# Graph attention with residual and layer norm on one core: the first adjacency columns are loaded ahead of x's last chunk, the row constant is made before the first scores, and masks are made later in periods 0 to 4

## What is computed

```python
q = x @ Wq.T + bq
k = x @ Wk.T + bk
v = x @ Wv.T + bv
scores = q @ k.T / sqrt(128)
scores = where(adj > 0, scores, -9e15)      # adj is 4096 x 4096 int32
att = softmax(scores, axis=-1) @ v
out = layernorm(x + elu(att))
```

## Time and profile before

| | |
|---|---|
| time, median of 3 runs | 429.18 us (428.96 to 430.1) |
| the profiled execution's own time | 429.98 us |
| its span | 428.2 us |
| busy: PE, PEld (weight loads) | 415.1 us (97%), 310.7 us |
| busy: DVE, ACT, POOL | 361.7 us (84%), 353.8 us (83%), 353.5 us (83%) |
| HBM read, written | 69.47 MB, 2.10 MB |

### The profile page before, as it was taken

The page is one execution under the profiler, slowest core; times in us unless marked ns, Lnnn a source line. Parts: engine busy times, 40 slices in busy tenths (PEclk is TensorE's granted clock), DMA queues, the critical chain, the costliest instruction groups (busy, mean ns, idle before and its releaser), DMA issues.

```text
span 428.2 us, 11461 instructions
## 1 busy us (share of the span) xinstructions
PE 415.1 (97%) x3470; PEld 310.7 (73%) x3470; DVE 361.7 (84%) x677; ACT 353.8 (83%) x742; POOL 353.5 (83%) x644
## 2 busy tenths in 40 slices
PE   7897999999999999999999999999999999999994
PEld 6663777777777777777777777777777777777784
DVE  3698999888888898888888988888889888888784
ACT  5887778988888889888888898888888988888892
POOL 0588469888898898888988988889888988898875
PEclk9999999999999999999999999999999999999998
DMA  8953999999999999999999999999999999999551
GB/s 229 383 199 63 266 251 282 268 260 273 281 250 265 277 262 257 251 283 261 251 257 283 263 256 252 277 263 261 251 280 261 261 246 281 263 258 233 104 97 27
DMA packets 149649, 104.77 MB, mean 245 GB/s; under 512 B 132738, under 2 KB 141444, under 8 KB 141444
## 3 DMA queue, kind: packets, MB, share of 16 engines
q1 hardware_dynamic: 149200, 104.41, 91.6%
q10 hardware_dynamic: 436, 0.20, 0.2%
HBM read 69.47 MB, written 2.10 MB: 167 GB/s over the span
## 4 chain that ended last, share of the span: by engine, by line
POOL 58%; issue 18%; PE 11%; ACT 3%; DVE 3%; POOLq 2%; DMA 2%; SPq 2%; ACTq 0%; DVEq 0%
POOL p_rows L403 26%; POOL res L417 6%; POOL var_eps L439 4%; POOL rstd L441 4%; POOL y L422 3%; POOL att_sum L410 3%; POOL neg_mean L428 3%; PE ps_out L960 3%; POOL att L412 3%; POOL expm L419 2%; POOL centred L430 2%; DMA adj<-in_adj_dram 2%; POOL y_out L445 2%; PE ps_out L962 1%; PE ps_t L937 1%
## 5 line engine op out<-in xcount | busy, mean ns | idle before, releaser
L403 POOL TENSOR_TENSOR p_rows<-scores,p_rows 128x256 f16<-128x256 f32 x252 | 177.1, 733 | 7.4 <-ACT p_rows L560 7.0
L687 DVE CUSTOM_DVE_ANT_0 scores<-ps_scores,adj 128x1024 f32<-128x1024 f32 x128 | 155.7, 1216 | 11.6 <-issue 8.6
L543 ACT ACTIVATE scores<-scores,neg_max 128x1024 f32<-128x1024 f32 x128 | 145.9, 1140 | 4.0 <-DVE neg_max L697 4.0
L673 DVE TENSOR_SCALAR adj<-adj 128x1024 f32<-128x1024 int32 x128 | 104.3, 816 | 2.5 <-DMA adj<-in_adj_dram 2.5
L703 DVE TENSOR_TENSOR p_lo<-ps_t,p_hi 128x512 f16<-128x512 f32 x124 | 82.4, 684 | 28.4 <-ACT p_hi L552 28.3
L921 PE MATMUL ps_scores<-k_hi,q_hi 128*128 128x512 f16 x256 | 97.1, 379 | 1.1 <-DVE max_parts L687 0.7
L922 PE MATMUL ps_scores<-k_lo,q_hi 128*128 128x512 f16 x256 | 97.0, 379 | 0.0
L923 PE MATMUL ps_scores<-k_hi,q_lo 128*128 128x512 f16 x256 | 97.0, 379 | 0.0
L960 PE MATMUL ps_out<-v_parts,p_hi 128*128 128x256 f16 x496 | 95.1, 273 | 0.0
L960 PE MATMUL ps_out<-v_parts,p_turned 128*128 128x256 f16 x496 | 95.0, 273 | 0.0
L962 PE MATMUL ps_out<-v_parts,p_lo 128*128 128x128 f16 x496 | 88.5, 219 | 0.0
(11 more groups left out here) (121 smaller groups left out, 477.0 us busy)
## 6 DMA issues: line engine op xcount, KB each, us to landing
adj<-in_adj_dram SPq DMA_DIRECT2D x64, 1024.0 KB, 5.3
out_dram<-y_out SPq DMA_DIRECT2D x32, 64.0 KB, 4.8
x_rows<-in_x_dram SPq DMA_DIRECT2D x4, 256.0 KB, 4.6
x_rows<-in_x_dram SPq DMA_DIRECT2D x2, 512.0 KB, 7.1
p_turned<-p_rows SPq DMA_TRANSPOSE x63, 4.5
w_rows<-in_L_gnn_Wq_dram ACTq DMA_DIRECT2D x1, 64.0 KB, 2.8
w_rows<-in_L_gnn_Wk_dram ACTq DMA_DIRECT2D x1, 64.0 KB, 3.4
w_rows<-in_L_gnn_Wv_dram ACTq DMA_DIRECT2D x1, 64.0 KB, 4.6
```

The lines of the kernel that those rows point to most:

```text
L403: last = nc.gpsimd.tensor_tensor(p_rows[c][:, w:][:, cols], s_sb[s][:, c * PIECE:c * PIECE + w][:, cols], p_rows[c][:, 0:w][:, cols], ALU. ...
L543: nc.scalar.activation(s_sb[s][:, cols], s_sb[s][:, cols], ACT.Exp, bias=neg_max[:, s:s + 1], accum_out=p_sums[:, s, c:c + 1]).then_inc(ex ...
L673: nc.vector.tensor_scalar(mask_sb[s][:, cols], adj_sb[s][:, cols], 0.0, MASKED / SCALE, ALU.is_le, ALU.mult).then_inc(mask_ready, 1)
L687: nc.vector.tensor_tensor_reduce(out=s_sb[s][:, cols], in0=ps_scores[c % 2][:, :], in1=mask_sb[s][:, cols], scale=SCALE, scalar=-3.0e38, o ...
```

## The change

On SP, the first five x chunks are issued, then columns 0 to 1023 and 1024 to 2047 of tile 0 as two loads of 512 KB, then x's last chunk, then the other three adjacency halves of tiles 0 and 1, and bv last. On DVE and PE, the constant of the rows (`bk_wide`, the product, `row_b`) comes before PE's `transpose_x(4)`. On DVE, the mask and the masking of piece 0 of tile 0 come before `low_of_k(4)`. From period 0 to period 4 a table says which mask pieces follow each masked piece; period 4 and 5 are written out, and the loop begins at period 6.

```diff
+X_EARLY = 5
...
-            for n, (begin, end) in enumerate(X_CHUNKS):
+            def load_x(n):
+                begin, end = X_CHUNKS[n]
                 tiles = slice(begin * BLOCKS, end * BLOCKS)
                 sp.dma_start(x_rows[:, tiles, :], x_tiled[:, tiles, :]).then_inc(x_in[n], 16)
-            sp.dma_start(bv_rows[:, :], bv.rearrange("(a d) -> a d", a=1).to_broadcast([P, D])).then_inc(bv_in, 16)
...
-            load(0, 0)
-            load(1, 1)
+            for n in range(X_EARLY):
+                load_x(n)
+            sp.dma_start(adj_sb[0][:, 0:PIECE], adj_tiled[0, :, 0:PIECE]).then_inc(adj_first, 16)
+            sp.dma_start(adj_sb[0][:, PIECE:2 * PIECE], adj_tiled[0, :, PIECE:2 * PIECE]).then_inc(adj_in[0][0], 16)
+            for n in range(X_EARLY, len(X_CHUNKS)):
+                load_x(n)
+            load_half(0, 0, 1, True)
+            for h in range(2):
+                load_half(1, 1, h, True)
+            sp.dma_start(bv_rows[:, :], bv.rearrange("(a d) -> a d", a=1).to_broadcast([P, D])).then_inc(bv_in, 16)
...
             def mask_piece(i, s, c):
 
                 cols = slice(c * PIECE, (c + 1) * PIECE)
-                dve.wait_ge(adj_in[s][c // 2], 8 * (i - s) + 16)
+                if isinstance(i, int) and i == 0 and c == 0:
+                    dve.wait_ge(adj_first, 16)
+                else:
+                    dve.wait_ge(adj_in[s][c // 2], 8 * (i - s) + 16)
...
-                    if j % 2 == 1 and has_scores:
+                    if j % 2 == 1 and has_scores and (warm or p > 0 or j > 1):
                         masked_piece(p, n, j // 2, not warm and p < 2)
...
             low_of_k(0)
+            dve.wait_ge(b_copied, 1)
+            nc.vector.tensor_copy(bk_wide[:, :], b_cols[:, 1:2].to_broadcast([P, P])).then_inc(wide_set, 1)
             dve.wait_ge(fold_ready, 2)
             nc.vector.tensor_copy(bq_k[:, 0:1], ps_fold[:, FOLD_B]).then_inc(fold_copied, 1)
             nc.vector.tensor_scalar(wv_t[:, D:D + 1], ps_fold[:, WR], -SCALE, None, ALU.mult).then_inc(row_copied, 1)
             low_of_k(1)
             low_of_q(0)
-            dve.wait_ge(b_copied, 1)
-            nc.vector.tensor_copy(bk_wide[:, :], b_cols[:, 1:2].to_broadcast([P, P])).then_inc(wide_set, 1)
+            dve.wait_ge(row_ready, 1)
+            nc.vector.tensor_scalar(row_b[:, 0:1], ps_fold[:, ROW_B], -SCALE, None, ALU.mult).then_inc(row_copied, 1)
             for g in (2, 3):
                 low_of_k(g)
-            dve.wait_ge(row_ready, 1)
-            nc.vector.tensor_scalar(row_b[:, 0:1], ps_fold[:, ROW_B], -SCALE, None, ALU.mult).then_inc(row_copied, 1)
+            mask_piece(0, 0, 0)
+            masked_piece(0, 0, 0, True)
             low_of_k(4)
-            mask_piece(0, 0, 0)
             low_of_k(5)
-            period(0, 0, has_1=False, has_2=False, warm=False, rows_at={5: 0})
-            period(1, 1, has_2=False, warm=False, rows_at={6: 1})
-            period(2, 0)
-            period(3, 1)
-            with dve.Fori(2, TILES // 2 - 1) as pair:
+            period(0, 0, has_1=False, has_2=False, warm=False, rows_at={5: 0},
+                   masks=(((0, 1),), ((0, 2), (0, 3)), ((1, 0),), ((1, 1),)))
+            period(1, 1, has_2=False, warm=False, rows_at={6: 1},
+                   masks=(((1, 2),), ((1, 3),), (), ((2, 0),)))
+            period(2, 0, masks=(((2, 1),), ((2, 2),), ((2, 3),), ((3, 0),)))
+            period(3, 1, masks=(((3, 1),), ((3, 2),), ((3, 3), (4, 0)), ((4, 1),)))
+            period(4, 0, masks=(((4, 2),), ((4, 3), (5, 0)), ((5, 1),), ((5, 2),)))
+            period(5, 1)
+            with dve.Fori(3, TILES // 2 - 1) as pair:
...
             transpose_x(3)
+            pe.wait_ge(wide_set, 1)
+            pe.wait_ge(fold_copied, 2)
+            pe.wait_ge(row_copied, 1)
+            nc.tensor.matmul(ps_fold[:, ROW_B], bk_wide[:, :], b_cols[:, 0:1], start=True, stop=True).then_inc(row_ready, 1)
             transpose_x(4)
...
                             transpose_x(5)
-                            biases_product()
```

More of the change, by code:

```diff
@@ L158, in attention_kernel @@
         adj_in = [[sem(f"adj_in{n}_{h}") for h in range(2)] for n in range(2)]
+        adj_first = sem("adj_first")
         mask_ready = sem("mask_ready")
@@ L302, in load_half @@
                 sp.dma_start(adj_sb[slot][:, cols], adj_tiled[i, :, cols]).then_inc(adj_in[slot][h], 16)
-            def load(i, slot):
-                for h in range(2):
-                    load_half(i, slot, h, True)
             def store(i, slot):
@@ L762, in finish_last, with period @@
                                         ALU.subtract, ALU.mult).then_inc(last_done, 1)
-            def period(p, n, has_scores=True, has_1=True, has_2=True, warm=True, makes_mask=True, rows_at={}):
+            def period(p, n, has_scores=True, has_1=True, has_2=True, warm=True, makes_mask=True, rows_at={}, masks=None):
                 for j in range(STEPS):
@@ L777, in period @@
                         reciprocal(p - 2, n)
-                    if has_scores and not warm and p == 0:
-                        for c in ((1,), (2, 3), (), ())[j // 2] if j % 2 == 1 else ():
-                            mask_piece(0, 0, c)
-                        for c in ((), (), (0,), (1, 2))[j // 2] if j % 2 == 1 else ():
-                            mask_piece(1, 1, c)
+                    if masks is not None:
+                        for i, c in masks[j // 2] if j % 2 == 1 else ():
+                            mask_piece(i, i % 2, c)
                     elif has_scores:
@@ L892, in _ @@
             transpose_x(3)
+            pe.wait_ge(wide_set, 1)
+            pe.wait_ge(fold_copied, 2)
+            pe.wait_ge(row_copied, 1)
+            nc.tensor.matmul(ps_fold[:, ROW_B], bk_wide[:, :], b_cols[:, 0:1], start=True, stop=True).then_inc(row_ready, 1)
             transpose_x(4)
-            def biases_product():
-                pe.wait_ge(wide_set, 1)
-                pe.wait_ge(fold_copied, 2)
-                pe.wait_ge(row_copied, 1)
-                nc.tensor.matmul(ps_fold[:, ROW_B], bk_wide[:, :], b_cols[:, 0:1], start=True, stop=True).then_inc(row_ready, 1)
             def scores(i, j, first):
```

## The result

| | before | changed |
|---|---|---|
| median, timed together (20 runs each) | 430.12 us (428.96 to 431.84) | 428.97 us (427.82 to 430.13) |
| the profiled execution | 429.98 us, span 428.2 | 428.14 us, span 426.4 |

The ratio is 0.9973, 95% interval 0.9964 to 0.9982: 1.15 us (0.8 to 1.5) less. The profiled pair differs by 1.84. I had forecast 2.5, and 426.7 us. The time is missed by 2.3 us: 0.94 of that is the base, since the three runs of before that I started from had a median of 429.18 and the twenty beside the changed kernel 430.12. The rest, 1.35, is the gain.

A forecast was written before the change was run, and what follows sets the result against it. PE was taken as the bound, with only its time through the first 42 us open to gain. 1.6 + 1.1 - 0.2 = 2.5 us off the median 429.18 gave 426.7 us, own range 425.9 to 427.2, overall 425.8 to 428.2.

The forecast's parts named there:

- start: PE up to `project_q(1)`: waits for `row_b` and `low_of_k(5)` go, ACT is late next; 1.6 us gained.
- later masks: End of period 1: without the mask piece ahead of `p_lo`, PE's second transposes come 1.1 us sooner.
- turned tiles and POOL: First values of tile 0: turned tiles come only 2.0 us sooner against PE's 2.7; 0.2 us off, between 0 and 0.7.
- rival 2: POOL and the turns eat up to all of the later 1.1 us; total gain 1.6, 427.6 us; chance 0.13.
- rival 3: Both gains fall short, or an unseen middle wait gives back the start's; gain 0.5, 428.7 us; chance 0.09.
- the wait before the first `transposes`: Tile 0's first transposes waiting for `q_lo`: the 1.1 us stay, since period 1 has as many masks ahead.
- the 0.2 "to spare": At `transpose_x(6)`: PE comes at 13.7 us, x's last chunk at 13.5, so no wait, with 0.2 us margin.
- Rival 1: First adjacency quarter lands late, at 12.5 us; start gains 0.5 to 1.0, total 1.6 to 2.1, about 427.4; chance 0.12.
- the row constant moves all by 0.62: Third step of scores: without the wait for `row_b`, everything behind 11.73 us moves up by 0.62.
- From about 42 us on PE runs through: After the start PE has no waits until the very end, so each microsecond gained earlier should stay to the end.

The follow-up runs named there:

- turn first: Changed kernel with tile 3's first half load issued behind tile 0's second turn: 427.73 us, 0.9956 of before; timed again 427.49 us, 0.9931.
- bv and turn: Kernel before with bv's load behind the first four adjacency halves and tile 3's first half load behind tile 0's second turn: 429.55 us, 0.9973.
- masks later: Kernel before with only the table of mask pieces for periods 0 to 4 changed: 429.81 us, 1.0013 of before.
- Hold later: Changed kernel with `row_neg` of tile 1 made two steps later, in period 2: 428.36 us, 0.9966 of before.
- changed 2: The changed kernel run again without any edit, for a second profile: 428.78 us, 0.9950 of before.
- all three: Changed kernel with x's last chunk between the quarters, tile 3's first half load behind the second turn, tile 1's `row_neg` two steps later: 428.90 us, 0.9952.
- bv last: Kernel before with only bv's load moved behind the first four adjacency halves: 428.87 us, 0.9972 of before.
- loads only: Kernel before with only the changed kernel's order of loads on SP, including the two quarters: 429.22 us, 0.9985 of before.
- row early: Kernel before with only `bk_wide`, its product and `row_b` made ahead of the first scores: 430.51 us, 1.0012 of before.

## Why the prediction was wrong

Means over the three profiles of each kernel, against the terms of the sum:

| term | predicted | measured | steps |
|---|---|---|---|
| start | 1.6 | 1.36 | 0 to 14: 26.11 to 24.75 |
| later masks | 1.1 | 0.82 | 14 to 17: 6.54 to 5.72 |
| turned tiles and POOL | -0.2 | -0.86 | 17 to last: 362.71 to 363.57 |
| sum | 2.5 | 1.32 | |

The 1.32 lies between my rival 2 (1.6) and my rival 3 (0.5).

**The step that failed** is the third, "I take 0.2 off for these, between 0 and 0.7". It measured 0.86, as much as the later masks gave. That is rival 2 (all of the later gain eaten up, 427.6), by its mechanism: PE waits for `p_turned` or ACT's late `p_rows`. Most of it is in steps 24 to 25, 0.48 (1.74 to 2.22), then 0.20 in 17 to 24 and 0.15 in 25 to 39. I had looked at the first turn, which was even with PE as worked out, and said of the second only that it "is also only 2.0 ahead". Its row in the trace before was there to be read: ACT already waited 1.26 for it, and the turn took 8.7 us from 41.35 behind an adjacency half issued at 40.20. ACT came to it 2.3 sooner (48.67 - 2.12 for 50.12 - 1.26) and the turn landed 1.5 sooner, so the wait had to grow by 0.8, and did: 2.12. That it is the order in SP's queue is shown by turn first, which brings exactly the 1.74 back on the changed kernel, with and without the other edits (four profiles of four; on the kernel before, bv and turn, it is 1.80); and that the masks set it off by masks later, alone with 2.16. The waits for turned tiles in steps 17 to 24 and 25 to 39 came in two profiles of three, and what makes them come is not shown.

**The later masks** were mis-sized as well. At `p_lo`, the wait that I had put at 1.1, the three profiles of each kernel agree: 1.09, 1.09 and 1.10 before, 0.49, 0.49 and 0.50 after, so 0.6. The other 0.5 went to a term that I had left out: `row_neg` stood ahead of `p_lo` in both orders, but took 0.17 before and 0.70 here beside POOL. Hold later gets the 0.6 back and gives 0.24 of it up again by step 24. The rest of the measured 0.82 is luck: the wait before the first `transposes`, which I said would stay, fell from 1.09, 1.08 and 0.75 to 0.75, 0.75 and 0.74. One profile of the kernel before has the low value too, and the cause is not shown.

**The start** was right in mechanism. bv is the cause: 0.77 to 1.2 us with it alone, and nothing left of the gain without it. What is missing from the 1.6 comes mostly from having read one profile. The wait at `transpose_x(7)`, 1.20 in the profile that I started from, was 0.92 and 0.72 in the other two of the kernel before. The changed kernel reached what I had worked out for steps 0 to 4 (7.92 - 1.8 = 6.1) in two profiles of three (6.09 and 6.14). In the first, the first quarter landed at 11.3 and not 10.7, x's last chunk at 14.4 and not 13.5, and `transpose_x(6)` waited 0.51; the 0.2 "to spare" was too thin for that execution. Rival 1, a first quarter at 12.5, is not what usually happens, but single executions (12.2 in changed 2, 13.0 in all three) come near it. That the row constant moves all by 0.62 is right only when the mask comes early: alone it gave nothing.

**"From about 42 us on PE runs through, so a microsecond that PE gains before then should stay to the end"** is too strong. PE's slack to the turned tile of tile 4 was 0.28 us in the kernel before (landed 92.29, used 92.57), and bv last, loads only and row early each show a wait there. Why the DMA transpose takes 6 to 9 us at some turns and 4.3 to 5.5 at others was not settled: in the case that I looked at, the load ahead of it was late.

## What to carry to other kernels

PE "busy for all of its time" says that it has no gap, not that its inputs have slack: before a gain is summed to the end, subtract landing from use for each transfer of the next periods, and take the smallest as what the gain may be. Where an engine off the path already waits for a transfer, a gain ahead of it lengthens that wait by all that the transfer does not come sooner (2.3 against 1.5 us here), so the order in the queue (transpose ahead of the bulk load) is changed with the gain. And where executions differ by as much as the change is worth, one pair of profiles is a draw: three of each, cut at fixed places of the program, show which stretches agree (from step 39 to the last, all six lie within 0.06 us) and which waits come and go.

## What the runs showed of the hardware

- A broadcast load of one 512-byte row to 128 partitions, 64 KB, held up the loads queued behind it: a 1 MB load landed 3.7 to 4.2 us behind the x chunk ahead of it with the broadcast between them (five profiles), 2.5 without (two, bv last and bv and turn). The bytes of the broadcast at 426 GB/s are 0.15.
- A DMA transpose queued right behind a 1 MB load (the second of tile 0) took 8.5 to 9.6 us to land in every profile with this order, the first of tile 0, with none ahead, 4.4 to 4.9. With the load put behind it, the second took 5.8 to 6.6 (five profiles).
- The same loads of the start landed up to 2.4 us apart between executions: the first quarter, behind the same five chunks, at 10.6 to 13.0. Where the two quarters were queued one behind the other, their distance stayed at 1.3 to 1.5.
- A VectorE operation on 29 columns (`row_neg`) took 0.70 to 0.72 us in the nine profiles in which it fell into GpSimd's `low_rows`, and 0.16 to 0.17 in the seven in which these had ended.
